# A four-layer graph network on one core: mask sums packed a stage earlier through one buffer, and VectorE casts in place of reloaded tiles

## The reference

```python
# layer 0: per-node weights from an embedding, hops 0, 1, 2
w = jnp.einsum('nd,dkio->nkio', embedding, weight)
As = [eye, A, 2.0 * (A @ A) - eye]
x = layernorm(x + einsum('bnki,nkio->bno', einsum('knm,bmc->bnkc', A_stack, x), w) + b)
# layer 1: twice z = relu((A z) W_i)
x = layernorm(x + z)
# layer 2: x W_self + (A x) W_neighbor + bias
x = layernorm(x + out_self + out_neighbors + bias)
# layer 3: x, A x, 2 A (A x) - x for two supports (both are adj), concatenated, times one weight
x = layernorm(x + x_cat @ weight + bias)
```

## Time and profile before

| | us |
|---|---|
| median of 3 runs | 1213.95 (1209.44 to 1216.85) |
| the profiled execution, its own time | 1218.93 |
| its span in the profile | 1217.1 |
| stages j = 0, 1, 2, 3 (T's first to last) | 107.2 to 208, 211.5 to 339.3, 342.8 to 471.5, 475 to 578 |
| passes n0 to n8 begin at | 617, 674.3, 736.6, 799.6, 861.4, 927, 993.1, 1062.1, 1140.3 |

### The profile page before, as it was taken

How to read it: one execution, slowest core, us unless ns; L and a number is a source line. 1 busy time by engine, 2 the same in 40 slices (tenths; PEclk the granted TensorE clock), 3 DMA queues, 4 the chain that set the end, 5 groups by cost and what they waited for, 6 DMA issues and landing times.

```text
span 1217.1 us, 16608 instructions
## 1 busy us (share of the span) xinstructions
PE 1173.1 (96%) x5539; PEld 969.2 (80%) x5539; DVE 813.3 (67%) x1773; ACT 509.2 (42%) x687; POOL 336.5 (28%) x208
## 2 busy tenths in 40 slices
PE   9999999999999999899999999999999999988996
PEld 6888888888888887777888787888888887866875
DVE  5935897877768877998347357788657574733544
ACT  6622111120111101110156666677666766743665
POOL 0001111010105553654121113244536241410312
PEclk9999999999999999999999999999999999989998
DMA  9832112241214221221543454525654166687563
GB/s 364 328 104 62 40 45 73 64 102 34 62 60 113 70 70 44 82 66 52 172 180 139 158 174 149 170 98 158 150 139 121 34 152 163 162 221 215 170 218 107
DMA packets 181453, 154.77 MB, mean 127 GB/s; under 512 B 121520, under 2 KB 141520, under 8 KB 180080
## 3 DMA queue, kind: packets, MB, share of 16 engines
q1 hardware_dynamic: 170272, 113.24, 31.3%
q10 hardware_dynamic: 11088, 40.38, 10.4%
HBM read 109.01 MB, written 44.56 MB: 126 GB/s over the span
## 4 chain that ended last, share of the span: by engine, by line
PE 78%; DVE 8%; DMA 5%; SPq 5%; issue 2%; ACT 1%; POOL 0%; POOLq 0%; DVEq 0%; ACTq 0%
PE ps L1630 20%; PE ps L1207 15%; PE ps L1209 15%; PE ps L1517 8%; PE ps L1518 8%; PE ps L1535 7%; SPq L1447 4%; DMA B<-tf 3%; PE ps L1565 2%; PE ps L1566 2%; DVE nat L1937 2%; DVE ring L1937 2%; DMA ring_g<-td 1%; DVE xs L1916 1%; SPq L1495 1%
## 5 line engine op out<-in xcount | busy, mean ns | idle before, releaser
L1207 PE MATMUL ps<-B,ops 128*128 128x512 f32 x1008 | 403.8, 401 | 13.8 <-DMA B<-tf 11.8
L1209 PE MATMUL ps<-B,ops 128*128 128x512 f32 x1008 | 395.3, 392 | 0.0
L1259 ACT CAST B<-pk 128x1024 fp32r<-128x1024 fp8e4 (+1 forms) x266 | 262.1, 1020 | 139.7 <-PE ps L1209 136.0
L1630 PE MATMUL ps<-Tw,xs 128*128 128x512 f32 x1280 | 309.6, 391 | 7.6 <-DVE ring L1937 7.3
L1630 PEld LDWEIGHTS ps<-Tw,xs 128*128 128x128 f32 x1280 | 238.2, 188 | 64.7 <-DVE ring L1937 9.6
L1207 PEld LDWEIGHTS ps<-B,ops 128*128 128x128 f32 x1008 | 191.0, 189 | 59.6 <-DMA B<-tf 17.9
L1209 PEld LDWEIGHTS ps<-B,ops 128*128 128x128 f32 x1008 | 191.0, 189 | 36.8
L1517 PE MATMUL ps<-B,xs 128*128 128x512 f32 x512 | 200.3, 391 | 0.7 <-DVE xs L1838 0.7
L1518 PE MATMUL ps<-B,xs 128*128 128x512 f32 x512 | 199.3, 389 | 0.0
L1937 DVE SCALAR_TENSOR_TENSOR nat<-ps,embn,nat 128x128 f32<-128x128 f32 x448 | 152.8, 341 | 40.6 <-PE ps L1630 39.9
L1937 DVE SCALAR_TENSOR_TENSOR ring<-ps,embn,ring 128x128 f32<-128x128 f32 x512 | 174.3, 340 | 0.0
(11 more groups left out here) (121 smaller groups left out, 1191.7 us busy)
## 6 DMA issues: line engine op xcount, KB each, us to landing
B<-tf ACTq DMA_DIRECT2D x77, 512.0 KB, 3.6
raw<-in_at SPq DMA_DIRECT2D x10, 1024.0 KB, 15.2
td<-raw SPq DMA_DIRECT2D x33, 256.0 KB, 2.6
tf<-B SPq DMA_DIRECT2D x15, 512.0 KB, 2.6
raw<-in_at SPq DMA_DIRECT2D x12, 512.0 KB, 8.7
zd<-nat SPq DMA_DIRECT2D x24, 256.0 KB, 3.0
stg<-zd SPq DMA_DIRECT2D x24, 256.0 KB, 5.2
tb<-stq SPq DMA_DIRECT2D x40, 128.0 KB, 2.2
```

The source lines that it names most:

```text
L1207: pe.matmul(bank, ops[:, slot, 0, m, :], of, start=not more and m == 0, stop=False, skip_group_check=more)
L1209: mm = pe.matmul(bank, ops[:, slot, 1, m, :], of, start=False, stop=m == 7, skip_group_check=more)
L1259: eng.copy(to, of).then_inc(s_exA, 1)
L1630: mm = pe.matmul(ps[:, 4 + 2 * p + q, :], src, Tw[:, wi, 512 * p:512 * p + 512], start=i == 0, stop=i == 4)
```

## The change

Four parts. (1) Builds and builts stand in the stages j = 1 and 2 instead of 2 and 3, a built one tick behind its build instead of two, five of them in eight ticks instead of seven. (2) `stq` is one buffer of 1 KB, laid where W1 will lie; every build after the first waits for the store before it; W1 is loaded again in tick 4 of stage 3 ("weights1"), behind the last two stores, and `s_c2` counts 64 for those that use it. (3) `EXPANDS` has 40 letters a kind: kind 3 goes from 15 D and 25 A in a pass to 6 D, 11 V and 23 A; kind 4 from 10 D and 30 A to 6 D, 5 V and 29 A; kind 6 from 15 D and 25 A to 15 V and 25 A (12 V in n8, whose last eight pieces are A); kinds 2 and 5 are the same as before. Over the nine passes D goes from 77 to 24, V from 25 to 84, A from 266 to 260, and six pieces instead of 15 are stashed. (4) In the last pass the last chunk's weigh stands at slot 28 instead of 29, and the very last unit is a multiply on DVE instead of POOL. The new lines of the code shift the numbers: L1259, L1263, L1292 and L1296 become L1263, L1267, L1296 and L1300, the casts, loads and forms; L1399 to L1407 become L1405 to L1413; L1962 and L1972 become L1975 and L1985.

```diff
@@ weave
-            for t in range(40) if fast and j > 1 else ():
-                if 32 * (j - 2) + i == 6 + 7 * t // 5:
+            for t in range(40) if fast else ():
+                if 32 * (j - 1) + i == 1 + 8 * t // 5:
                     put("build", t)
-                if 32 * (j - 2) + i == 8 + 7 * t // 5:
+                if 32 * (j - 1) + i == 2 + 8 * t // 5:
                     put("built", t)
+            if fast and (j, i) == (3, 4):
+                put("weights1")
@@ tables
-EXPANDS = {2: "AAVAAVAV", 3: "AADAADAD", 4: "AADAAAAD", 5: "AAAAAAAV", 6: "AADAADAD"}
+EXPANDS = {2: "AAVAAVAV" * 5, 3: "DDDAAVAAVAAVAAVADDDAAVAAVAAVAAVAAVAAVAAV", 4: "DDDAAAAAAVAAAAAVDDDAAAAAAVAAAAAVAAAAAVAA", 5: "AAAAAAAV" * 5, 6: "AAVAAVAVAAVAAVAVAAVAAVAVAAVAAVAVAAVAAVAV"}
-STASHED = [k for k in range(40) if EXPANDS[6][k % 8] == "D"]
+STASHED = [k for k in range(40) if "D" in (EXPANDS[3][k], EXPANDS[4][k], EXPANDS[6][k])]
-LAST_WEIGH = [17, 18, 21, 22, 25, 26, 27, 29]
+LAST_WEIGH = [17, 18, 21, 22, 25, 26, 27, 28]
@@ buffers
-            stq = sb("stq", [P, 2, 1024], F8, scope)
...
+        with ExitStack() as scope:
+            stq = sb("stq", [P, 1024], F8, scope)
         W1 = sb("W1", [P, 2, P], F32)
@@ weigh on PE
-                            pe.wait_ge(s_c2, 48)
+                            pe.wait_ge(s_c2, 64)
@@ the root's reciprocal on DVE
+                        if s == last_unit:
+                            dv.wait_ge(s_rec, unit2_at[s])
+                            dv.tensor_tensor(g, g, sm[:, 0, :].unsqueeze(2).to_broadcast([P, 8, C]), ALU.mult).then_inc(s_a2, 1)
@@ build on POOL
-                        to, had = stq[:, t % 2, :], stq[:, 1 - t % 2, :]
+                        to, had = stq[:], stq[:]
-                        if t > 1:
-                            po.wait_ge(s_st[t % 2], had_st + 16 * (t // 2))
-                        else:
-                            po.wait_ge(s_lo, split_at[Step("split", 3, 0, 3)])
-                            po.wait_ge(s_hi, split_at[Step("split", 3, 0, 3)])
                         if t > 0:
+                            po.wait_ge(s_st[(t - 1) % 2], had_st + 16 * ((t + 1) // 2))
                             po.wait_ge(s_build, t)
+                        else:
+                            po.wait_ge(s_B, len(tile_at))
+                            po.wait_ge(s_c2, 48)
@@ built and weights1 on SP
+                    if s.kind == "weights1":
+                        for i in range(2):
+                            sp.wait_ge(s_st[i], had_st + 16 * 20)
+                        sp.dma_start(W1[:], wbd[:, 0:2, :]).then_inc(s_c2, 16)
```

More of the change, by code:

```diff
@@ L488 @@
 AHEAD = {4: 7, 5: 5}
-LAST_WEIGH = [17, 18, 21, 22, 25, 26, 27, 29]
+LAST_WEIGH = [17, 18, 21, 22, 25, 26, 27, 28]
 def expander(e):
-    return EXPANDS[PASSES[e // 40][1]][e % 8] if e < 40 * len(PASSES) - 8 else "A"
+    return EXPANDS[PASSES[e // 40][1]][e % 40] if e < 40 * len(PASSES) - 8 else "A"
 def chunks(n):
@@ L606, in second_part @@
     return {t: [s for _, s in sorted(of, key=lambda e: e[0])] for t, of in events.items()}
-LATER = {s.kind for of in second_part().values() for s in of if s.kind != "sums"} | {"build", "built"}
+LATER = {s.kind for of in second_part().values() for s in of if s.kind != "sums"} | {"build", "built", "weights1"}
 GENERAL, FAST = order(False), order(True)
@@ L659, in gnn_stack @@
             glo = sb("glo", [P, 512], F32R, scope)
-        with ExitStack() as scope:
-            stq = sb("stq", [P, 2, 1024], F8, scope)
         ring_g = sb("ring_g", [P, 512], F32)
@@ L1016, in second_way @@
                 dev_at, unit2_at = (numbered(FAST, kind, start=first_var) for kind in ("deviation", "unit"))
+                last_unit = max(unit2_at, key=unit2_at.get)
                 turn2_at = numbered(FAST, "flip", "yflip", start=len(turn_at))
@@ L1387, in pool_step @@
                         m, o = divmod(t, 5)
-                        to, had = stq[:, t % 2, :], stq[:, 1 - t % 2, :]
+                        to, had = stq[:], stq[:]
                         b11, b12 = (B[:, m, 1024 * h:1024 * h + 1024].bitcast(F32) for h in range(2))
                         b21, b22 = (B[:, 8 + m, 1024 * h:1024 * h + 1024].bitcast(F32) for h in range(2))
-                        if t > 1:
-                            po.wait_ge(s_st[t % 2], had_st + 16 * (t // 2))
-                        else:
-                            po.wait_ge(s_lo, split_at[Step("split", 3, 0, 3)])
-                            po.wait_ge(s_hi, split_at[Step("split", 3, 0, 3)])
-                        if t > 0:
-                            po.wait_ge(s_build, t)
+                        if t > 0:
+                            po.wait_ge(s_st[(t - 1) % 2], had_st + 16 * ((t + 1) // 2))
+                            po.wait_ge(s_build, t)
+                        else:
+                            po.wait_ge(s_B, len(tile_at))
+                            po.wait_ge(s_c2, 48)
                         if o == 0:
@@ L1430, in pool_step @@
                             po.tensor_tensor(to, home_half(2 * g, 0), home_half(2 * g + 1, 0), ALU.subtract).then_inc(s_raw, 1)
-                    if s.kind == "unit":
+                    if s.kind == "unit" and s != last_unit:
                         sm, g = stats(j, c), home(j, c).rearrange("p (g k) -> p g k", k=C)
@@ L1456, in sp_step @@
                         sp.wait_ge(s_build, s.j + 1)
-                        sp.dma_start(tb[[0, 1, 3, 2, 4][o], :, 1024 * m:1024 * m + 1024], stq[:, s.j % 2, :]).then_inc(s_st[s.j % 2], 16)
+                        sp.dma_start(tb[[0, 1, 3, 2, 4][o], :, 1024 * m:1024 * m + 1024], stq[:]).then_inc(s_st[s.j % 2], 16)
+                    if s.kind == "weights1":
+                        for i in range(2):
+                            sp.wait_ge(s_st[i], had_st + 16 * 20)
+                        sp.dma_start(W1[:], wbd[:, 0:2, :]).then_inc(s_c2, 16)
                     if s.kind == "zload":
@@ L1500, in sp_step @@
                     if s.kind == "ship":
-                        sp.wait_ge(s_norm, unit2_at[s._replace(kind="unit")])
+                        if s._replace(kind="unit") == last_unit:
+                            sp.wait_ge(s_a2, len(plus_at) + 1)
+                        else:
+                            sp.wait_ge(s_norm, unit2_at[s._replace(kind="unit")])
                         sp.dma_start(out[j, :, cols], home(j, c)).then_inc(s_h[j][c], 16)
@@ L1598, in pe_steps @@
                         if p in (2, 3):
-                            pe.wait_ge(s_c2, 48)
+                            pe.wait_ge(s_c2, 48 if general else 64)
                             mm = pe_weighed(pe, bank, c, (y, W1[:, p - 2, :]))
```

## The result

The changed kernel takes 1199.81 us (median of 4 runs, 1198.62 to 1201.24) against 1214.53 before (4 runs, 1209.44 to 1216.85): 14.7 us less, ratio 0.9878, 95% interval 0.9857 to 0.9899. Its profiled execution took 1200.17 us with a span of 1198.3, so it stands at its median, where the profiled execution of before (1218.93) stood 4.4 us above this one of four runs and 5.0 above that of the three shown ahead of the prediction.

A forecast was written before the change was run, and what follows sets the result against it. The prediction took TensorE (PE, 96% busy) to bound the kernel, so only its waits and lower clock could be won. Terms summed to -20.7 us, profiled 1218.93 to 1198, less a carried-over 5.0: 1193 us, range 1181 to 1214.

The forecast's parts named there:

- which I carry over: Last step of the sum: the profiled execution's 5.0 us above the median is kept, taking 1198 to 1193 us.
- the term for the builds in stages 1 and 2: Stages 1 and 2: DVE's idle time and preparation cover hide the packs and single buffer; +1 us, bounds 0 and +4.
- n7: Pass n7, layer six: casts replace loads that PE waits for and that delay transposes; -10 us, bounds -3 and -15.
- n8: Pass n8, layer six: 12 casts replace loads and remove PE's waits; -2 us, bounds 0 and -2.7.
- kinds 3 and 4: Passes n1 to n4: fewer loads, some late casts; -4 us for kind 3, +0.5 us for kind 4.
- the tail: End of the last pass: last multiply on DVE instead of POOL, last plus one slot earlier; -0.7 us.
- Builds out of the last stage: Stage 3: without packs DVE's operations are no longer stretched and PE stops waiting for them; -5.5 us.
- the first rival: n7's transposes stay late in SP's serial queue, casts eat n1's and n2's gain; about 8 us gained, 1206; chance 0.20.
- The stash: Pass n0: stashing six pieces instead of 15 does not matter, since no wait stands there; no size given.
- the second: Rival: all 59 added casts delay work PE awaits, 44 us against 25.5 of gains; 1233 us; chance 0.07.
- The third: Rival: POOL instructions lock out DVE's casts in the passes; 6 us less gain, 1199 us; chance 0.09.
- The fourth rival: Stages 1 and 2: with one buffer, packs and a store delay preparations in POOL's queue, 30 us; 1223 us; chance 0.06.

The follow-up runs named there:

- only6: The kernel before with one edit, the 27 loads of kind 6 turned into VectorE casts: 1202.34 us, ratio 0.9885.
- u_34: The changed kernel with the EXPANDS tables of kinds 3 and 4 as before: 1203.61 us, ratio 0.9907.
- u_place: The changed kernel with the packs back in stages 2 and 3 and the double buffer: 1201.22 us, ratio 0.9889.
- p_lock: The changed kernel with its packs at other ticks, none in ticks 12 to 15 of stages 1 and 2: 1197.96 us, ratio 0.9867.
- p_three: The changed kernel with 8 packs in stage 0, 16 in each of stages 1 and 2, none there in ticks 3-6 and 12-15: 1195.04 us, ratio 0.9847.
- t_refill: p_three with SP's refill loads issued behind the transposes' reads of the same slot instead of ahead: 1189.85 us, ratio 0.9791.
- u_34b: The same kernel as u_34, timed on another chip beside the changed kernel: 1202.55 us, ratio 0.9896.

## Why the prediction was right, and where it was off

The forecast was 1193 us in a range of 1181 to 1214, faster by over 1% with 0.62. The measured 1199.8 lies within it, and 14.7 us are 1.2%. The mechanism named as the largest, the loads of layer six, was the largest: only6 has 13.8 us from these casts alone. The 6.8 us by which the forecast was too fast have two sources.

*The first is the step "which I carry over": that the 5.0 us by which the profiled execution stood above the median would stay.* The forecast for the profiled execution was 1198.2 us and it took 1200.2, only 2.0 us off. But after the change the profile stands at its median (0.4 above it), so 4.6 of the 6.8 us are the carry-over. How far a profile stands from its median is chance: in the kernels here it runs from 3.1 us below (u_34) to 2.5 above (u_place). The executions of before differ with what their loads cost: n1 and n2 took 62.30 and 63.00 us in the profile, 60.6 and 60.9 with the same tables in only6, 59.4 and 60.5 in u_34. That the whole of the 5 us was due to loads that the change removes is not shown. But a sum of waits read from a slow execution belongs to that execution; taken off a median 5.0 us lower, it counts waits that the median does not have.

*The second is the term for the builds in stages 1 and 2: +1, bounds 0 and +4; it was +5.9 (3.5 and 2.4) by the two profiles, and 4.3 against only6, where stages 1 and 2 took 127.9 and 130.2.* That DVE had some 30 us of idle time in stage 1 was taken as cover. It is no cover where PE waits for DVE soon after: p_lock took the split's wait away, and p_three, with more stretched work than before the change but no packs at these places, had 128.7 and 127.9 us. The other half, a store that waits in SP's queue ahead of a fetch, had been named; it was priced against the cover of a preparation (6.6 us of the earlier trace rows), while what it hit was a store further back in the queue, `y1d<-ring`, whose landing DVE needed at once. PE's waits divide the term: 1.55 and 1.58 us behind held DVE operations, 1.0 and 0.8 behind SP's queue, in stages 1 and 2.

This term was off by 4.9 us, and yet the sum for the profile by only 2.0: stage 3, n7, n8, n0 and the kinds 3 and 4 brought 4.1 us more than forecast between them, the tail 1.2 to 1.6 less. That they take more than half of the miss away is luck.

The other terms, by the profiles:

- Builds out of the last stage: -5.5, measured -5.7. L1916's successor took 782 ns there, 1365 before, and DVE's busy time fell from 92.91 to 84.68.
- n7: -10, measured -10.7. The rest did stay in SP's queue, as the first rival said of the whole; t_refill shows that it was the place of the refills.
- n8: -2, measured -3.6 to the last weigh (65.6 to 62.0 us from the pass's beginning to its start), and -3.2 in only6.
- Kinds 3 and 4: -3.5 together, measured -4.2 by these two profiles (-3.0, -3.7, +2.0, +0.5), but nothing side by side in u_34b. The 2.2 us of late casts in n1 and in n2 were 0.7 each; n3, where the step had next to none, has 1.7, behind a form that waited for ACT, where the step named chunk work.
- The stash was set to nothing. n0 takes 56.4 us with six pieces stashed and 57.7 or 57.8 with 15, in u_34 and u_34b: 1.3 us that were not seen (0.9 against the 57.3 of before).
- The tail: -0.7, measured +0.5 to +0.9; the step compared a multiply on DVE alone with one on POOL, and left out that POOL was still at the one before.

Of the signs that it named, L1916 near 0.8 us, n7 near 68 us and n1 and n2 near 60 came. These did not: PE's waits for DVE's products from stage 3 to the handover are 2.3 us and not under 2, the clock of n7 is 0.97, the reads that PE waited for there landed in 4.5 us (median) and not near 3, and stages 1 and 2 are longer.

The rivals: the second needs 0.43 us of PE delay a cast; PE's matmuls waited 5.1 us for 84 casts, 0.06 each. The third was right in its rule and wrong in its place. The casts had a mean of 793 ns, 40 more than before, where it had 0.33 us for each; the split was held for 2 us. The Trainium skill states, page "SBUF — State Buffer", section "Who interferes with whom", that a DVE instruction with two SBUF inputs contends with a GpSimd instruction that reads SBUF. The trace agrees: the split reads two tiles in SBUF and the pack reads the mask there, and the split's 2.76 us end just after the pack. The prediction weighed that section for the casts alone. The fourth rival's mechanism, packs ahead of a preparation in POOL's queue, shows at none of the three preparations from 234 to 264 us, which each waited for ACT's cast; the delay by stores in SP's queue cost 1.0 and 0.8 us, of its 30.

## What to carry to other kernels

Idle time of an engine in a stage is cover only where nobody waits for its next result: before adding work that can hold it, find the few instructions of that stage whose result another engine needs within a microsecond, and put the new work elsewhere. An engine that issues both prefetches and results in one order wants the urgent ones first: moving four loads behind four reads took n7 from 67.3 to 62.6 us here, a third of what the change brought. And a profile's waits for DMA are one draw; take them from two or three profiles before a sum is made of them, and do not take a sum read from a slow profile off a faster median.

## What the runs showed that was not expected

A DVE operation of 128x8 elements, 0.17 us elsewhere, took 2.37 us beside a POOL instruction of 2.39 that began 0.05 us earlier, and a split of 0.69 took 2.76: by these rows a hold lasts to the end of the POOL instruction, for the small operation as for the large. On the other side a stretch in which PE has work throughout forgives a great deal: in p_three DVE was busy 101.03 instead of 96.18 us in stage 1, and the stage took 0.9 us more. And the four refills ahead of the reads cost n7 not only the 3.8 us of waiting but the clock: 0.97 in the changed kernel's n7, 1.00 in t_refill's, with 63.62 against 62.31 us of PE busy time for the same matmuls.
